# Turning the second expert product, turning router rows unscaled, and adding fetched rows two steps ahead in a fused transformer block

## What is computed

```python
x = x + 0.5 * ffn(layernorm(x))      # 16 experts, top 2, and a shared expert
x = x + attn(layernorm(x))           # attention and a mixture, below
x = x + 0.5 * ffn(layernorm(x))      # the first part again

def attn(x):
    a = x + (gated linear attention of rmsnorm(x) * scale1) @ Wo + bo    # chunks of 64 tokens
    xf = rmsnorm(a) * scale2
    probs = softmax(xf @ router_W + router_b)         # 8 experts
    top, idx = top_k(probs, 2);  top = top / top.sum()
    for e in range(8):                                # at most 640 token slots each
        h = gelu(xf[tok] @ W1[e] + b1[e]) @ W2[e] + b2[e]
        out[tok] += gate * h
    return a + out
```

## Time and profile before

| what | us |
|---|---|
| median of three runs (lowest, highest) | 752.68 (752.09, 754.5) |
| the profiled execution: its time, its span | 746.56, 744.8 |
| attention begins on DVE | 179.53 |
| rank2 begins on DVE | 354.32 |
| first gather, last scatter of the mixture begins | 372.55, 478.96 |
| front3 begins on DVE | 481.75 |
| busy: PE, POOL, DVE, ACT | 516.0, 421.1, 384.9, 287.2 |

### The profile page before, as it was taken

How to read it: one execution, slowest core, us unless ns; L and a number is a source line. 1 busy time by engine, 2 the same in 40 slices (tenths; PEclk the granted TensorE clock), 3 DMA queues, 4 the chain that set the end, 5 groups by cost and what they waited for, 6 DMA issues and landing times. The chain is left out here.

```text
span 744.8 us, 10789 instructions
## 1 busy us (share of the span) xinstructions
PE 516.0 (69%) x2860; PEld 395.4 (53%) x2860; DVE 384.9 (52%) x1192; ACT 287.2 (39%) x713; POOL 421.1 (57%) x444
## 2 busy tenths in 40 slices
PE   3889898885238899984169999525667469998600
PEld 3834787773126677863147877313333158887400
DVE  5874444442256999746712222068774225654317
ACT  4645444442234567633024242122544324443200
POOL 4413777772787784000077777418777517777730
PEclk9999999997556999985569999955887879999955
DMA  7260455552111120224011111153111323333248
GB/s 221 73 187 19 114 152 138 154 160 68 42 46 41 50 58 22 74 82 142 0 47 54 50 54 50 48 154 99 50 44 50 100 62 108 102 104 104 65 119 245
DMA packets 88518, 66.12 MB, mean 89 GB/s; under 512 B 10150, under 2 KB 80939, under 8 KB 88460
## 3 DMA queue, kind: packets, MB, share of 16 engines
q1 hardware_dynamic: 75596, 40.85, 19.3%
q0 software_dynamic: 11712, 24.04, 10.8%
q10 hardware_dynamic: 1152, 0.53, 0.2%
HBM read 36.63 MB, written 28.75 MB: 88 GB/s over the span
## 5 line engine op out<-in xcount | busy, mean ns | idle before, releaser
L1898 POOL DMA_INDIRECT ffn_pairs<-ffn_out,ffn_target x79 | 80.9, 1024 | 43.1 <-issue 21.6
L795 POOL DMA_INDIRECT ffn_rows<-norm_rows,core_gather_id x79 | 78.0, 988 | 39.3 <-issue 20.1
L299 POOL DMA_INDIRECT attn_back<-ffn_out_rows,core_back_slot x64 | 64.8, 1013 | 30.3 <-issue 18.4
L1651 POOL DMA_INDIRECT expert_rows<-front_norm,front_slot_int x64 | 62.1, 970 | 24.4 <-issue 18.4
L1541 ACT ACTIVATE moe_hid<-moe_hid_ps,core_b 128x320 f32<-128x320 f32 x64 | 33.5, 527 | 52.4 <-PE moe_hid_ps L1514 51.8
L1470 POOL DMA_INDIRECT moe_rows<-moe_rows,core_gather_id x40 | 39.0, 976 | 24.9 <-SPq L1447 13.0
L892 DVE TENSOR_TENSOR ffn_hid<-ffn_gate,ffn_gu_ps 128x256 f32<-128x256 f32 (+1 forms) x40 | 16.7, 417 | 65.0 <-ACT ffn_gate L873 64.9
L1480 POOL DMA_INDIRECT moe_pairs<-moe_out,core_scatter_id x40 | 39.0, 975 | 17.5 <-issue 11.6
L1526 PE MATMUL moe_out_ps<-core_moe_w,moe_hid 128*128 128x128 f32 x320 | 46.3, 288 | 0.0
L1990 DVE TENSOR_TENSOR ffn_hid<-ffn_gate,ffn_gu_ps 128x256 f32<-128x256 f32 (+1 forms) x40 | 16.7, 418 | 52.8 <-ACT ffn_gate L1971 52.8
L1925 PE MATMUL ffn_gu_ps<-core_gate_up,ffn_rows_t 128*128 x158 | 42.8, 394 | 0.5 <-ACT ffn_rows_t L1964 0.5
(11 more groups left out here) (275 smaller groups left out, 1354.7 us busy)
## 6 DMA issues: line engine op xcount, KB each, us to landing
ffn_rows<-expert_rows SPq DMA_DIRECT2D x79, 64.5 KB
ffn_out_rows<-ffn_out SPq DMA_DIRECT2D x39, 128.0 KB, 2.4
core_moe_w<-in_w SPq DMA_DIRECT2D x8, 512.0 KB
moe_pairs<-core_zero SPq DMA_DIRECT2D x4, 1024.0 KB
front_pair<-moe_pairs SPq DMA_DIRECT2D x8, 512.0 KB, 4.9
last_pair<-ffn_pairs SPq DMA_DIRECT2D x8, 512.0 KB, 5.9
core_x<-in_x SPq DMA_DIRECT2D x8, 256.0 KB, 4.8
norm_rows<-front_norm SPq DMA_DIRECT2D x8, 256.0 KB, 2.2
```

The lines of the kernel that those rows point to most:

```text
L299: pool.indirect_dma_start(out=self.got[j % self.depth][:, k, b, :], out_offset=None, in_=self.rows, in_offset=bass.IndirectOffsetOnAxis(ap ...
L795: pool.indirect_dma_start(out=rows[i % ring][:, h, :], out_offset=None, in_=core.norm_rows, in_offset=bass.IndirectOffsetOnAxis(ap=core.ga ...
L1651: pool.indirect_dma_start(out=core.expert_rows, out_offset=bass.IndirectOffsetOnAxis(ap=slot_int[:, j, g:g + 1], axis=0), in_=norm[j % rin ...
L1898: pool.indirect_dma_start(out=core.ffn_pairs, out_offset=bass.IndirectOffsetOnAxis(ap=target[:, n:n + 1], axis=0), in_=out[q % deep][:, h, ...
```

## The change

1. **Attention, added rows.** `added_in(i)` replaces i+3: rounds -3 and -2 add and measure steps 0 and 1 as before, round -1 none, and round i from 0 on step i+2. `ATTENTION_AHEAD`, how many gathers of the next step POOL issues before the roots of a step, goes from (3, 5, 5, 7, 8, ...) to (4, 5, 7, 8, 8, ...).
2. **Attention, ACT's order.** r1 of step i+2 moves from behind the squares to behind the copies of heads, values, gates and q.
3. **Router.** PE turns a1 itself (a1_t) instead of r2, and DVE multiplies the logits by the root that the rows were to be scaled by. r2 is still made, behind the copy of a1_t, and stored. The router bias is added when experts are chosen, on the logits directly: the softmax is gone. The two gates come from one exp of the difference of the two top logits, in rank2 (ACT), and three small DVE operations there.
4. **Mixture.** The second product has W2 as the loaded operand and the hidden values as the moving one: a half of 320 columns is four products into one bank. VectorE adds b2, now one value per partition, while it copies out to `out_t` (`keep`), PE turns the five tiles back (`turn_back`, after the fourth hidden product of the next expert), VectorE copies again and POOL scatters as before, in parts of two and three tiles.
5. **Loads.** b2 leaves the row of biases that front1 splits into three bf16 parts (1664 columns become 640) and is loaded with the weights of the mixture as 128x8.

```diff
-ATTENTION_AHEAD = (3, 5, 5, 7, 8, 8, 8, 8)
+ATTENTION_AHEAD = (4, 5, 7, 8, 8, 8, 8, 8)
-BIAS_COLS = 5 * D + MOE_EXPERTS * D
+BIAS_COLS = 5 * D
...
+        else:
+            @block.scalar
+            def _(act):
+                act.wait_ge(apart_ready, 1)
+                nc.scalar.activation(odds[:], apart[:], ACT.Exp).then_inc(odds_done, 1)
...
+            else:
+                nc.vector.tensor_tensor(apart[:], core.tops[:, 1, :], core.tops[:, 0, :], ALU.subtract).then_inc(apart_ready, 1)
...
+                vec.wait_ge(odds_done, 1)
+                link(nc.vector.tensor_scalar(whole[:], odds[:], 1.0, None, ALU.add))
+                link(nc.vector.reciprocal(core.moe_gates[:, 0, :], whole[:]))
+                nc.vector.tensor_tensor(core.moe_gates[:, 1, :], odds[:], core.moe_gates[:, 0, :], ALU.mult)
             vec.wait_ge(tokens_done, 1)
...
-                    if j >= 1:
-                        pool.wait_ge(sig["r2_ready"], j)
-                    pool.tensor_tensor(rms2[:], sum_sq[:], half[:, 0:BATCH], ALU.pow).then_inc(sig["rms2_ready"], 1)
+                    pool.tensor_tensor(rms2[:, j, :], sum_sq[:], half[:, 0:BATCH], ALU.pow).then_inc(sig["rms2_ready"], 1)
...
                     copy_out(q_t[:], "q_t", i)
+                j = i + 2
+                if within(j):
+                    act.wait_ge(sig["rms1_ready"], j + 1)
+                    for b in range(BATCH):
+                        last = nc.scalar.activation(r1[j % 2][:, b, :], core.x[:, b, j, :], ACT.Identity,
...
-                    copy_out(r2_t[:], "r2_t", i - 2, core.norm2[:])
-                    if i - 2 == S - 2:
-                        exp_logits(0)
...
+                    copy_out(a1_t[:], "a1_t", j, core.norm2[:])
+                    act.wait_ge(sig["rms2_ready"], j + 1)
...
+                        last = nc.scalar.activation(r2[j % 2][:, b, :], core.a1[:, b, j, :], ACT.Copy, scale=rms2[:, j, b:b + 1])
...
+            added_in = lambda i: -1 if i == -1 else i + 3 if i < 0 else i + 2
...
+                    vec.wait_ge(sig["rms2_ready"], j + 1)
                     ring.await_filled(vec, "logits", j)
...
-                        spread(core.router_bias[:], BATCH, inner=False), ALU.add)
+                        spread(rms2[:, j, :], MOE_EXPERTS), ALU.mult)
...
-                if within(i + 3):
-                    back.add(nc, vec, core.x[:, :, i + 3, :], i + 3)
+                j = added_in(i)
+                if within(j):
+                    back.add(nc, vec, core.x[:, :, j, :], j)
                 if within(i):
                     state_after(i, 0)
-                if within(i + 3):
-                    measure(i + 3)
+                if within(j):
+                    measure(j)
...
-                    pe.wait_ge(sig["r2_ready"], i - 2)
-                    turn("r2_t", i - 3, lambda b: r2[(i - 3) % 2][:, b, :])
+                    ring.await_emptied(pe, "wo", i - 3)
+                    turn("a1_t", i - 3, lambda b: core.a1[:, b, i - 3, :])
...
+            def turn_back(e):
+                for k, (lo, hi) in enumerate(back_parts):
+                    pe.wait_ge(out_kept, 2 * e + k + 1)
+                    if e + 1 < MOE_EXPERTS:
+                        pe.wait_ge(turn_copied, 2 * (e + 1) + k + 1)
+                    for t in range(lo, hi):
+                        last = nc.tensor.transpose(t_ps[k][:, (t - lo) * D:(t - lo + 1) * D], out_t[:, t * P:(t + 1) * P], core.c("ident"))
+                    last.then_inc(returned, 1)
+            def second(e, h):
+                pe.wait_ge(gelu_done, len(units) * e + HID_CHUNKS * (h + 1))
...
+                    last = nc.tensor.matmul(out_ps[h][:, 0:half], core.w2[:, e, c, :], hid[e % 2][:, c, h * half:(h + 1) * half],
+                                            start=(c == 0), stop=(c == HID_CHUNKS - 1))
...
+                    if u == turn_after and e >= 1:
+                        turn_back(e - 1)
+                second(e, 0)
                 if e + 1 < MOE_EXPERTS:
                     turn(e + 1)
...
+                second(e, 1)
+            turn_back(MOE_EXPERTS - 1)
...
+                if e >= 1:
+                    copy_out(e - 1)
+                keep(e, 0)
                 if e + 1 < MOE_EXPERTS:
                     copy_turned(e + 1)
...
+                keep(e, 1)
+            copy_out(MOE_EXPERTS - 1)
```

More of the change, by code:

```diff
@@ L972, in plan @@
         for i in range(first, end):
-            for what, j in (("q_t", i - 1), ("r1_t", i + 1), ("r2_t", i - 3), ("wo", i - 2), ("logits", i - 3), ("out_t", i - 1)):
+            for what, j in (("q_t", i - 1), ("r1_t", i + 1), ("a1_t", i - 3), ("wo", i - 2), ("logits", i - 3), ("out_t", i - 1)):
                 if within(j):
@@ L1004, in attention @@
         r2 = [s.sb(f"r2_{k}", [P, BATCH, D]) for k in range(2)]
-        r2_t = s.sb("r2_t", [P, BATCH * P])
-        probs = s.sb("probs", [P, BATCH, S, MOE_EXPERTS])
+        a1_t = s.sb("a1_t", [P, BATCH * P])
         same = s.sb("same", [P, BATCH, S, MOE_EXPERTS])
-        most, total, inverse = (s.sb(n, [P, BATCH, S]) for n in ("most", "total", "inverse"))
+        first_of = s.sb("first_of", [P, BATCH, S])
         choice_parts = (slice(0, S - 2), slice(S - 2, S))
@@ L1121, in _ @@
                     last.then_inc(sig["sums_ready"], 1)
[L1122 to L1138, removed]
                 if within(i - 1):
@@ L1172, in _ @@
                     last.then_inc(sig["ln_ready"], 1)
-            exp_logits(1)
         @block.vector
@@ L1200, in rotary @@
                 nc.vector.tensor_tensor(two(sin_part), by_head, sin_of(i), ALU.mult).then_inc(sig["qk_read"], 1)
[L1202 to L1209, removed]
             def choose(k):
                 here = choice_parts[k]
[L1214 to L1220, removed]
-                        [by_step(core.moe_pick[q])[:, :, here, :] for q in range(2)],
[L1222 to L1227, removed]
+                ring.await_emptied(vec, "logits", here.stop - 1)
+                logits = by_step(core.logits[:])[:, :, here, :]
+                bias = core.router_bias[:].unsqueeze(1).unsqueeze(1).to_broadcast(list(logits.shape))
+                link(nc.vector.tensor_tensor(logits, logits, bias, ALU.add))
+                top_two(nc, link, logits, core.c("rev")[:, 0:MOE_EXPERTS],
+                        [by_step(core.moe_pick[q])[:, :, here, :] for q in range(2)],
+                        [tops[:, q, :, here] for q in range(2)], (same[:, :, here, :], first_of[:, :, here]))
             def state_after(j, c):
@@ L1444, in moe_experts @@
     assert MOE_EXPERTS == SEQ_TILES
-    split = 3
-    parts = ((0, split), (split, CAP_TILES))
+    parts = ((0, 3), (3, CAP_TILES))
+    back_parts = ((0, 2), (2, CAP_TILES))
+    turn_after = 3
     with Scope(nc, tag) as s, nc.Block(no_gpsimd_drain=True) as block:
@@ L1456, in moe_experts @@
         stored = [s.sem(f"stored{k}") for k in range(2)]
-        turned, turn_copied, hid_done, gelu_done, out_done, out_copied = (
-            s.sem(n) for n in ("turned", "turn_copied", "hid_done", "gelu_done", "out_done", "out_copied"))
+        turned, turn_copied, hid_done, gelu_done, out_done, out_kept, returned, out_copied = (
+            s.sem(n) for n in ("turned", "turn_copied", "hid_done", "gelu_done", "out_done", "out_kept", "returned", "out_copied"))
         units = [(c, h) for h in range(2) for c in range(HID_CHUNKS)]
-        assert half <= split * P
+        assert half <= parts[0][1] * P and back_parts[0][1] * P <= half
         @block.gpsimd
@@ L1553, in copy_turned, with keep, copy_out @@
                                             ).then_inc(turn_copied, 1)
+            def keep(e, h):
+                vec.wait_ge(out_done, 2 * e + h + 1)
+                if e >= 1:
+                    vec.wait_ge(returned, 2 * e)
+                nc.vector.tensor_scalar(out_t[:, h * half:(h + 1) * half], out_ps[h][:, 0:half], core.b2[:, e:e + 1], None, ALU.add
+                                        ).then_inc(out_kept, 1)
+            def copy_out(e):
+                for k, (lo, hi) in enumerate(back_parts):
+                    vec.wait_ge(returned, 2 * e + k + 1)
+                    if k == 0 and e >= 2:
+                        vec.wait_ge(stored[e % 2], 16 * CAP_TILES * (e // 2))
+                    nc.vector.tensor_copy(out[e % 2][:, lo:hi, :], t_ps[k][:, 0:(hi - lo) * D].rearrange("p (t d) -> p t d", d=D)
+                                          ).then_inc(out_copied, 1)
             copy_turned(0)
```

71 lines of the change are left out of this document (32 added, 39 removed).

## The result

The changed kernel takes 779.23 us (median of 4 runs, 778.67 to 784.75); beside it the kernel before took 752.38 (750.96 to 754.5). The ratio is 1.040 (95% interval 1.035 to 1.044; the two medians alone give 1.036): slower by 27 us, where +22 and 775 us were forecast, with 761 to 788 as the range. The profiled execution took 779.05 us, with a span of 777.3. One later execution of the kernel before, of 863 us at a mean granted clock of 0.623, is left out of every comparison.

What follows compares the result with a forecast made beforehand. DVE was taken to bound mid-attention, POOL's gathers its start, and PE to set the mixture's pace. Attention +25.7, its tail -3.2, mixture +1.0 and front -1.4 summed to +22.1, so 775 us, range 761 to 788.

Steps and rivals of the forecast that it cites:

- The wait: Mid-attention: the added rows' late turn delays DVE's denominators from T+4.54 to T+8.76 (T: end of measure), 4.22 us per step.
- The clock: Attention: PE's idle time before the turn lowers its clock, 1.7 us per step, +8.5 over five; bounds 0 and 4.8.
- rival (c): Attention: PE runs the whole path at 1.2 GHz, 790.3 us, or DVE holds POOL, up to 785; chance 0.16.
- (a): Attention: the wait is covered and only the earlier start remains; 743.7 us, faster; chance 0.09.
- (b): Attention: the clock stays at 2.4 GHz in the steps; 766.3 us; chance 0.15.
- (e): Attention: the wait is about 1.5 us and all cancels; 752 us; chance 0.05.
- The start: Attention's step 0: its phi comes 5.4 us earlier and its end on DVE 7.6 us earlier.
- Rounds with an add: Attention, end of step 0 to end of step 5: step 5 has an add too, 67.9 against 65.7 us, +2.2.
- The sixth round and the tail: Attention's sixth step: +1.5 us (between 0 and 4.2); its tail: SP's wait for other engines goes, -3.2 (bounds 0 and -3.2).
- Mixture and front: Mixture: first scatter later, end shorter, about +1 us (-5.9 to +3); first front: smaller bias split, -1.4.
- rival (d): The mixture does gain what PE saves, 6.9 less, 768 us; counted inside the summed forecast's chance of 0.55.
- The base: Whole kernel: +22 was put on the runs' median, 752.7 us, not the profiled execution's 746.56, giving 775.

Runs made afterwards that it cites:

- clock_kept: The changed kernel with 32 more turns of a constant on PE while it waits for the rows of steps 2 to 7; 761.96 us, ratio 1.013.
- before_again: The kernel before, unchanged, run and profiled a second time; 752.55 us, ratio 1.001, its profiled execution 755.22 us.
- few_before: The kernel before with only two of five scatters per expert in the mixture; 11.23 us per expert, 100.3 us from first gather to last scatter.
- turn_behind: The changed kernel with PE's late turn behind the last numerators, and ScalarE's exp and copy ahead of r2 and kept rows; 737.21 us, ratio 0.982.
- turn_only: The changed kernel with PE's late turn behind the last numerators, ScalarE's order kept except an earlier copy of a1_t; 756.98 us, ratio 1.008.

## Why the prediction was right, and where its sum was off

**The wait: right.** The mechanism, its place and its size are as forecast: the turn of attn_r is late by root, offset and normalising, PE works in order, DVE waits for attn_kv_ps. 4.22 was forecast per round, 4.5 is what clock_kept shows. The turn comes at T+4.32, not T+3.93, and that is POOL's offset: it took 0.74 and ended with DVE's line 1250, where the same instruction took 0.20 in a round of before:

```profile
268.31 0.20 POOL L1072 TENSOR_TENSOR attn_offset_pair<-attn_neg_mean,attn_root_pair 128x8 f32<-128x8 f32 x1
```

The root just ahead of it, beside line 1248, took 1.68, as with DVE idle. In the sixth round the offset began 0.05 us ahead of line 1250 and took 0.20. The Trainium skill (GPSIMD Engine Reference, section 1, Specifications) says that POOL's SBUF interfaces are shared with VectorE, with contention by DVE instructions that have two SBUF inputs. For the offset the trace agrees with it, for the root it doesn't; I had taken 0 and 1.7 as the bounds for each round.

**The clock: the step that was mis-sized.** I took 1.7 per round from one place where PE had waited 1.85 us, 8.5 in five rounds. Measured, by the start of the denominators beyond T+8.76, are 1.8, 3.0, 4.2, 4.1 and 4.2, together 17.3, of which 0.3 each is the later turn; in the first two less stands in PE's queue. clock_kept shows that the rest is the clock: its denominators come at T+9.07 in the round shown, and its five rounds take 91.1 us together where those of the changed kernel take 107.3, so the clock costs 16.2 us in place of 8.5. The row was of a wait half as long, and of it I had taken the slow part of five microseconds; here PE did nearly the whole path that DVE waits for at 1.2 GHz. That is rival (c), which I had priced at 3.1 more per round; it came with 2.2 more (4.2 less 0.3 and 1.7) in the last three. (a), (b) and (e) are refuted by the same rows.

**The start: right**, -8.6 for -7.6; counted from attention's start, step 0's phi came 6.3 earlier, not 5.4. **Rounds with an add:** +2.2 was forecast for the one more; 41.6 less five waits of 4.22 and 17.3 leaves 3.2.

**The sixth round and the tail: right in sum only roughly.** In the sixth round PE waits 3.94 us before the turn and does what follows at a clock of 0.50; the denominators come at T+12.4 where they came at T+7.2 before: 5.2 more, not 1.5. SP's wait for other engines went from 3.2 to 0.2, as forecast. The tail gave back 2.6 more (0.4 + 5.2 - 3.0), which was not forecast. It is found between the denominators of the last two steps. The same 62 instructions of PE are recorded there in the kernel before, in the changed kernel and in before_again:

```profile
319.46:333.48 14.02, 11.46 (x62) 9.12 (x62) 5.64 (x12) 4.32 (x17) 1.01 (x1) 0.76 0.32 93
...
357.00:368.29 11.29, 8.73 (x62) 7.07 (x62) 5.64 (x12) 4.49 (x18) 1.01 (x1) 1.00 0.39 117
...
323.75:340.93 17.18, 15.07 (x62) 11.91 (x62) 5.64 (x13) 5.32 (x21) 1.04 (x2) 0.56 0.25 76
```

The stretch is the longer the lower the clock, and the unchanged kernel alone had 14.02 and 17.18. The 2.7 us that the changed kernel gains here are thus not shown to come from the change. Together -0.4 instead of -1.7, and that is luck: two misses that cancel.

**Mixture and front: right.** +0.9 for +1.0, by the steps forecast: a later first scatter and a shorter end. PE's saving per expert is 1.5, not 1, and rival (d), that it shows, is refuted. The prediction's reading that PE sets the mixture's pace in the kernel before is wrong for the middle of the stage: an expert takes 12.7 us there, which are ten issues of POOL without a gap, and 11.23 when POOL has fewer (few_before). The terms of the sum did have POOL as the floor. front1 is 2.4 us shorter where DVE begins rank1 (39.84 after 42.22), but at attention's start 0.7 are left of it. The second profile of before has 41.25 and 180.32, so there the gain is 1.4 and 1.5: the 2.4 and the 0.7 hold a spread of about 1 us between executions.

**The base.** The sum, +22, is 10 too small against the profile that it was made on, +32.5. That 775 is yet only 4 below the median is in part luck, and due to where I put it on: on the median of the runs, 752.7, while the profiled execution had been 6 us quicker than that, in attention's clock for the most part (before_again). Its rows were those of a good execution. Against the span of the second profile of before, 753.5, the changed kernel's is 23.8 longer; the difference of the medians is 26.9.

## What to carry to other kernels

When work is moved later on one engine, look in the queue of the engine that consumes it at what stands behind the consumer, and move that ahead: with the order changed on both PE and ScalarE the same late rows cost nothing (turn_behind, 0.982), on PE alone the wait moved on (turn_only, 1.008). A wait of several microseconds on PE is to be priced with the half clock behind it: here 1.5 to 3.9 us in a round, behind waits of 2.6 to 4.5 us. A saving on an engine that isn't the bound of its stage is found by giving the bound room; here it was worth nothing until then. And one profile is one execution: before a sum is worked out from its rows, they are to be held against a second one.

## What was not expected of the hardware

After an idle time of 4.5 us the granted clock was 0.50 all the time from the turn at 292.46 to about 300.6, in which PE worked almost without a gap; in the five rounds it stayed there for 7 to 10 us from the turn on. 32 turns of a constant in that idle time (3.71 us of work) kept the clock at 0.99 to 1.00 in the five rounds, and with no other edit they made the program 17 us shorter.
